# Three products with V in one group, and one diagonal selected a step earlier, in an attention and mixture-of-depths layer

## What is computed

```
scores = jnp.einsum('bhki,bhqi->bhkq', k, q) / math.sqrt(HEAD)
mask = jnp.arange(n)[:, None] <= jnp.arange(n)[None, :]
scores = jnp.where(mask, scores, jnp.float32(-10000.0))
attn = jax.nn.softmax(scores, axis=2)
combined = jnp.einsum('bhkq,bhkl->bhql', attn, v)
```

## Time and profile before

| | |
|---|---|
| median of 3 runs | 2603.3 us (2601.86 to 2606.7) |
| profiled execution | 2603.97 us |
| its span | 2602.2 us |
| TensorE busy | 2507.7 us, 96% |
| VectorE busy | 1665.0 us, 64% |
| GpSimd busy | 1600.0 us, 61% |
| ScalarE busy | 1234.6 us, 47% |
| chain that ended last | TensorE 55%, GpSimd 34%, ScalarE 4% |
| mean granted clock of TensorE | 0.983 |

### The profile page before, as it was taken

How to read it: one execution, slowest core, us unless ns; L and a number is a source line. 1 busy time by engine, 2 the same in 40 slices (tenths; PEclk the granted TensorE clock), 3 DMA queues, 4 the chain that set the end, 5 groups by cost and what they waited for, 6 DMA issues and landing times.

```text
span 2602.2 us, 40583 instructions
## 1 busy us (share of the span) xinstructions
PE 2507.7 (96%) x13920; PEld 1821.6 (70%) x13920; DVE 1665.0 (64%) x4231; ACT 1234.6 (47%) x2354; POOL 1600.0 (61%) x1666
## 2 busy tenths in 40 slices
PE   7899999999999999999999999998999999999998
PEld 5565666667666667666667666674588888888886
DVE  6666667667767767777676677667465535544533
ACT  2555566566665666665666565665631111111110
POOL 1676788887888787888787888887241213122211
PEclk8998999999999999999999999998999999999999
DMA  7556567676666866657676576764430101011010
GB/s 144 91 97 129 115 151 167 127 152 145 139 143 126 171 141 137 155 130 141 127 181 126 119 175 127 142 130 131 155 106 33 33 25 41 17 30 36 17 33 17
DMA packets 167263, 286.46 MB, mean 110 GB/s; under 512 B 23121, under 2 KB 58001, under 8 KB 165906
## 3 DMA queue, kind: packets, MB, share of 16 engines
q1 hardware_dynamic: 159890, 267.01, 47.6%
q0 software_dynamic: 7168, 16.85, 2.0%
HBM read 116.97 MB, written 65.11 MB: 70 GB/s over the span
## 4 chain that ended last, share of the span: by engine, by line
PE 55%; POOL 34%; ACT 4%; issue 3%; DVE 2%; DMA 1%; SPq 0%; POOLq 0%; ACTq 0%; DVEq 0%
POOL Pa L786 29%; PE PS L1467 13%; PE PS L1446 13%; PE PS L1324 6%; PE PS L1412 5%; PE PS L1396 5%; PE PS L1365 4%; PE PS L1316 4%; PE PS L1330 2%; POOL Pm L763 2%; PE PS L1339 1%; POOL P L763 1%; ACT Pm L909 1%; DMA Kp<-nat 1%; POOL lnrs L799 1%
## 5 line engine op out<-in xcount | busy, mean ns | idle before, releaser
L786 POOL TENSOR_TENSOR Pa<-Pa,Pm 128x512 f32<-128x512 f32 (+1 forms) x623 | 770.9, 1258 | 153.7 <-ACT Pm L909 96.4
L1396 PE MATMUL PS<-Qp,Kp 98*128 98x512 f32 (+3 forms) x1536 | 550.9, 363 | 31.5 <-ACT Pm L909 13.1
L909 ACT ACTIVATE Pm<-PS 128x512 f32<-128x512 f32 (+3 forms) x856 | 395.4, 471 | 294.4 <-PE PS L1396 240.3
L1365 PE MATMUL PS<-Kp,Qp 96*128 96x512 f32 (+3 forms) x1536 | 500.6, 362 | 14.9 <-DMA Kp<-nat 5.1
L1006 DVE TENSOR_REDUCE nm<-PS 128x1 f32<-128x512 f32 x512 | 344.4, 685 | 193.2 <-PE PS L1365 192.5
L1396 PEld LDWEIGHTS PS<-Qp,Kp 98*128 98x128 f32 x1536 | 292.2, 192 | 241.8 <-ACT Pm L909 119.6
L786 POOL TENSOR_TENSOR Pa<-Pa,P 128x512 f32<-128x512 f32 (+1 forms) x307 | 381.8, 1263 | 73.3 <-ACT P L909 46.2
L876 ACT ACTIVATE G<-PS,b1c 128x512 f32<-128x512 f32 x128 | 88.2, 689 | 539.6 <-PE PS L1446 539.6
L1014 DVE CUSTOM_DVE_ANT_0 PS<-PS,maskA,nm 128x384 f32<-128x384 f32 (+3 forms) x512 | 263.3, 554 | 116.0 <-PE PS L1365 112.4
L1014 DVE CUSTOM_DVE_ANT_0 PS<-PS,maskA 128x384 f32<-128x384 f32 (+3 forms) x512 | 245.0, 506 | 137.9 <-PE PS L1365 137.9
L1365 PEld LDWEIGHTS PS<-Kp,Qp 96*128 96x128 f32 x1536 | 284.9, 195 | 68.4 <-DVE nm L1014 9.9
(11 more groups left out here) (142 smaller groups left out, 4261.9 us busy)
## 6 DMA issues: line engine op xcount, KB each, us to landing
Qp<-nat SPq DMA_DIRECT2D x192, 256.0 KB, 6.8
Kp<-nat SPq DMA_DIRECT2D x192, 256.0 KB, 5.7
o_s<-Of SPq DMA_DIRECT2D x64, 256.0 KB, 2.1
Ot<-o_s SPq DMA_DIRECT2D x64, 256.0 KB
xb<-in_x SPq DMA_DIRECT2D x64, 256.0 KB, 3.3
h_s<-hs SPq DMA_DIRECT2D x64, 256.0 KB, 3.4
out<-xb SPq DMA_DIRECT2D x64, 256.0 KB, 3.5
x_raw<-in_xt SPq DMA_DIRECT2D x15, 1024.0 KB, 6.4
```

The source lines that it names most:

```text
L786: e.tensor_tensor(to, to, probs(u, k)[:, h0:h0 + many, 0:w], ALU.add).then_inc(s["padd"], many)
L909: e.activation(probs(u, k)[:, h_, 0:w], PS[:, B_BANKS[j % 2], 0:w], ACT.Exp).then_inc(s["b_exp"], 1)
L1365: ins = e.matmul(to, Qp[0:96, u % 4, h_, qt * P:qt * P + P], Kp[0:96, (2 * i + k0 // 512) % 4, h_, 0:w], start=True, stop=True)
L1396: e.matmul(PS[:, B_BANKS[j % 2], 0:w], Kp[0:98, (2 * i + k // 4) % 4, h_, k % 4 * P:k % 4 * P + P], Qp[0:98, u % 4, h_, 512 - w:512], star ...
```

## The change

The three steps 1, 2 and 3 of a narrow unit become one group of products, in place of the groups (1) and (2, 3). How many beats a group lies behind its last scores is now read from a table, `PV_LAG`: as before for narrow step 0 and for all groups of wide units, and 2 in place of 3 for the narrow unit's last group. And in GpSimd's order the selection of a unit's last step stands ahead of the whole addition of the step before, in narrow and in wide units, and no longer between its two halves.

```diff
@@ -40,7 +40,8 @@
-PRODUCTS = (((0,), (1,), (2, 3)), ((0,), (1, 2), (3, 4), (5, 6, 7)))
+PRODUCTS = (((0,), (1, 2, 3)), ((0,), (1, 2), (3, 4), (5, 6, 7)))
+PV_LAG = ((3, 2), (2, 2, 3, 3))
@@ -241,8 +242,8 @@
             for k in range(ksteps(u)):
-                k1 = max([g for g in PRODUCTS[u % 2] if k in g][0])
-                n = self.formed[u, k1] + (2 if diag(u, k1) is None else 3)
+                j, k1 = [(j, max(g)) for j, g in enumerate(PRODUCTS[u % 2]) if k in g][0]
+                n = self.formed[u, k1] + PV_LAG[u % 2][j]
@@ -780,7 +781,7 @@
                         for h0 in range(0, HG, many):
-                            if h0 == 2 and kept_early(u, k + 1):
+                            if h0 == (0 if k + 2 == ksteps(u) else 2) and kept_early(u, k + 1):
                                 keep(u, k + 1)
```

## The result

The changed kernel takes 2594.61 us (median of 6 runs, 2589.82 to 2596.2) and the kernel before 2604.12 us (median of 6, 2601.86 to 2606.7): a ratio of 0.9959, with a 95% interval of 0.9946 to 0.9972. That is 9.5 us less where 20.8 were forecast. The profiled execution took 2595.95 us, 2594.2 of it span.

The account below looks back on a forecast made before the run. The prediction took a loop of sum, TensorE's stretch and GpSimd's run as the bound. Terms of 11.2 + 5.0 + 4.6 + 2.4 - 2.4 = 20.8 us gave 2583.2, as median 2582.5 us; range 2575 to 2596.

Parts of the forecast that it names:

- What bounds the kernel: Attention pairs: a loop of sum, some 21 us of TensorE, 33.5 us of GpSimd, sum; TensorE's own work a little shorter.
- One group less: TensorE, 32 narrow units: one way into and out of a group saved, 0.35 us each, 11.2 us (9.6 to 12.8).
- The slack in front of the sum: Between GpSimd's last addition and TensorE's sum: 0.20 of 0.26 us goes in 25 pairs, 5.0 us.
- The idle 0.17 us: GpSimd before step 6's first addition: the selection covers this wait, 0.15 us in 31 wide units, 4.6 us.
- The narrow group and its selection: Narrow unit's group one beat earlier, step 3's selection ahead of an addition: costs nothing, three us of margin.
- The copy: ScalarE's copy of products ahead of wide step 1's first exponential: 0.4 us in six pairs with split x, 2.4 us.
- The clock: TensorE's granted clock: low stretch slides in the first batch's four pairs, 2.4 us lost; rival of falls, above 2610, chance 0.07.
- Only the group counts: Rival: step 7's wait becomes an equal one at the sum, nothing loose is recovered; 11.2 us gained, 2592, chance 0.19.
- TensorE is the bound: Rival: the sum need not wait, so step 7's whole stall is won, 24 us on top of 11.2; 2568, chance 0.04.

Follow-up runs that it names:

- e10_heads: Changed kernel with the edits of e6_nudge and e7_hoist, and each GpSimd addition waiting only for its own head's previous addition: 2582.7 us, 0.9922 of the kernel before.
- e3_split: Kernel before with narrow steps 2 and 3 parted into two groups of products, 256 groups in place of 224: 2618.02 us, 1.0046 of the kernel before.
- e6_nudge: Changed kernel with the first score tile of the wide unit's step 0 a quarter of a beat later on TensorE: 2591.06 us, 0.9959 of the kernel before.
- e9_control: Kernel before with only the first score tile of the wide unit's step 0 moved later, as in e6_nudge: 2604.67 us, 1.0004 of the kernel before.
- e2_sel: Kernel before with only the earlier selection of a unit's last step, groups of products unchanged: 2599.12 us, 0.9974 of the kernel before.
- e7_hoist: Changed kernel with the selection of a unit's last step issued ahead of the addition's waits too: 2589.02 us, 0.995 of the kernel before.
- e4_lag3: Changed kernel with the narrow group of three one beat later, 3 in place of 2 beats behind its scores: 2592.52 us, 0.995 of the kernel before.
- e1_group: Changed kernel with the selection back at its old place, so the narrow group of three alone: 2602.25 us, 0.9988 of the kernel before.

## Why the prediction was right and where it was wrong

**What bounds the kernel: right.** The loop of sum, TensorE's stretch and GpSimd's run holds in every profile of the study; the period is the sum of its three parts each time, and e10_heads shows TensorE right below it, as "a little shorter than the loop" said.

**One group less: the failed step, by its size.** The price of a boundary, 0.35 us, was near (e3_split: 0.36; by the rows of this boundary 0.32, since the detour was 0.98 us and not 1.02). "It shortens the loop in full: 32 x 0.35 = 11.2 us" was wrong: the stretch became 0.14 us shorter, 4.5 us in all. The step looked at what TensorE does at the old place and not at what the detour gave others time for. ScalarE's exponential of step 3's last tile but one frees the place for the first wide tile, and TensorE now comes to that point before it is free; e6_nudge and e9_control show it, 0.15 us. Of the missing 0.21 the detour's size is 0.03 more, and 0.03 stay open. The lower bound of 9.6 us should have reached far further down: it came from the scatter of the price, while the earlier trace rows show that right behind the detour TensorE and ScalarE hand tiles of 128 columns to each other, 0.65 us of ScalarE's waiting for TensorE among them, and nothing said that this would bear 1.02 us less between them.

**The slack in front of the sum: right.** Forecast 0.20 us in 25 pairs; measured 0.21, by e2_sel alone about 5 us. The value came from the one place where the sum really waited, and not from the nearer but looser regular pairs.

**The idle 0.17 us: the second failed step.** "With the selection between them this wait is covered: 0.15 us", 4.6 us. Measured 0.05. The diff was read as "ahead of the addition", while it puts the selection behind the addition's wait. e7_hoist puts it ahead of that wait too and takes 0.15 us more: the mechanism was right and the code was misread.

**The narrow group and its selection: right in the 25 pairs.** The selection runs at 804.13, early enough; no product of a narrow group waits for it in the 25 pairs, and e4_lag3, with a beat more of margin, is no faster in them. In the first batch the earlier group does cost something, 1.5 us in one pair (below).

**The copy: size wrong.** 0.4 us a pair was right for ScalarE's row of work (0.39) and wrong for the period (0.08). The pairs with a split of x also scatter by waits for transfers, in either kernel. This one after stood 1.90 us, and its period was 59.14 us:

```profile
644.15 0.47 PE L1366 MATMUL PS<-Kp,Qp 96*128 96x512 f32 x1 [1.90 <-DMA Kp<-nat]
```

The kernel before had two such pairs, of 58.29 and 58.93 us, elsewhere. Together the six pairs take 347.5 us before and 345.8 after, 1.7 us less where 6 x 1.1 = 6.6 were summed.

**The clock: right in the regular pairs, a term that isn't there in the first batch.** In the regular pairs the waits of 0.25 us at the sum were followed by no fall: the mean granted clock from 352 to 1729 us is 1.00, as before. In the first batch 2.4 us were set against the 2.0 that the other terms give in its four pairs, and measured, these pairs gain 0.2 us. That is near the -0.4 of the sum, but by luck. At the place of the earlier trace rows the wait at step 7 has gone from 1.99 to 0.70 us, and the sum waits instead, a few products on:

```profile
288.37 0.43 PE L1413 MATMUL PS<-Pm,V 128*32 128x128 f32 x8 [0.70 <-POOL Pm L764]
...
292.19 1.94 PE L1340 MATMUL PS<-Pa,ones 128*32 128x512 f32 x8 [1.59 <-POOL Pa L787]
```

The sum's 1.94 us for 1.07 is work at the lower level of the clock (0.50 granted from 292.19 to 294.19), as before. But no more of it follows: over the 10 us behind the four sums the granted clock is 0.72, 0.71, 0.66 and 0.67 before and 0.72, 0.71, 0.68 and 0.68 after, and the stretches became shorter in all four pairs, by 0.18, 0.62, 0.33 and 0.33 us. What took this gain away is GpSimd's run in the second pair, 35.80 us before and 37.34 after. GpSimd waits longer for an exponential there, before and after:

```profile
214.66 1.28 POOL L786 TENSOR_TENSOR Pa<-Pa,Pm 128x512 f32<-128x512 f32 x1 [1.42 <-ACT Pm L909]
```

```profile
214.10 1.28 POOL L787 TENSOR_TENSOR Pa<-Pa,Pm 128x512 f32<-128x512 f32 x1 [2.77 <-ACT Pm L910]
```

This run is 37.0 to 37.4 us in every profile with the group of three at 2 beats, and 35.8 in e4_lag3, which has it at 3, and in e2_sel and e9_control, which don't have it. So it is a price of the group's earlier place, which the forecast had at nothing; how it comes about stays open.

**The sum of it.** Of the 20.8 us, 19.9 belonged to the 25 pairs, -0.4 to the first batch and 1.3 to the rest; measured at the last sum are 9.5, 0.2 and 2.0. The shortfall of 10.4 in the 25 pairs is 5.3 for the group (0.21 a pair: 0.15 for the cover that went with step 1's products, 0.03 for the detour's size, 0.03 open), 2.5 for the misread wait (0.10 a pair), 1.9 for the copy (0.32 in six), and 0.7 for the rest, the waits for transfers among it. *Of the rivals*, none happened. "Only the group counts" has the nearest time, but e1_group shows the group at 2.4 us and e2_sel shows the slack recovered, its opposite. "TensorE is the bound" came true only two steps on, in e10_heads, at 53.9 us a pair.

## What to carry to other kernels

Before an instruction is taken from a place on the engine that sets the time, look at what the others finish while it runs: the price of the detour is the most that can be gained, and how soon the next instruction behind it finds its buffer free decides how much of that arrives. When a step is moved ahead of another to cover that one's wait, look at where the wait is issued, not at where the work is. And read gains in the period of the steady loop, in its parts: here 0.05 us could be told there, while spans scattered by 4 us for reasons far away.

## What the runs showed of the hardware beyond what was expected

- A way into and out of a group of 128x32 products costs 0.36 us where TensorE sets the time (e3_split). The Trainium skill ("TensorEngine Tiling (Array Packing)", Key Properties) says that a change of tiling mode drains TensorE and gives no price; whether the 0.36 us are that drain alone no run here parts.
- An addition on GpSimd that waits for the end of the one right in front of it stands 0.17 us; a selection in this place stood 0.12. With a wait for an addition two or more back, there is no idle time (e10_heads: the run is 33.31 - 32.88 = 0.43 us shorter for the waits of a wide unit).
- GpSimd's selection of 512 columns takes 0.63 us, and 1.10 when an operation of VectorE with both inputs in SBUF is running as it begins (32 of 202 after, with no exception either way). Four of its additions take 5.02 us or 5.93, and a subtraction on VectorE 0.68 us or up to 1.82, by what the other engine does at the moment.
